# Sixteen row buffers, eight result buffers and sixteen-ahead gathers for the expert tiles, and head transposes tile by tile

## What is computed

```python
shared = silu_and_mul(x @ shared_gate_up_w.T) @ shared_down_w.T   # 704 wide
shared = shared * sigmoid(x @ shared_gate_w.T)
probs = softmax(x @ gate_w.T)
weights, chosen = top_k(probs, 2)
for e in range(8):
    w_e = where(chosen == e, weights, 0).sum(-1)
    combined += w_e[:, None] * (silu_and_mul(x @ w13[e].T) @ w2[e].T)   # 176 wide
out = shared + combined
```

## Time and profile before

| | us |
|---|---|
| median of 3 launches | 1727.43 |
| lowest and highest launch | 1725.33, 1733.93 |
| the profiled execution, its own time | 1732.21 |
| its span in the profile | 1730.4 |
| PE busy | 1476.0 (85%) |
| PE weight loads | 1110.5 (64%) |
| DVE busy | 912.3 (53%) |
| ACT busy | 754.0 (44%) |
| POOL busy | 411.3 (24%) |
| mean granted TensorE clock, share of full speed | 0.939 |

### The profile page before, as it was taken

One profiled execution on the slowest core, in us unless ns is written; L12 is line 12 of the kernel. 1 busy time (PEld: TensorE's weight loads), 2 busy tenths in 40 slices (PEclk: granted clock), 3 DMA queues, 4 the chain that ended last, 5 costly groups with the idle time before them and its releaser, 6 DMA issues. The chain is left out here.

```text
span 1730.4 us, 27960 instructions
## 1 busy us (share of the span) xinstructions
PE 1476.0 (85%) x10106; PEld 1110.5 (64%) x10112; DVE 912.3 (53%) x1968; ACT 754.0 (44%) x1872; POOL 411.3 (24%) x328
## 2 busy tenths in 40 slices
PE   6999999995799789999899879878887787898587
PEld 4777787874576667767676657665555566533466
DVE  5766665663731846565555563176554314376712
ACT  5565656561334333433434434433443342586242
POOL 2607061210235221110201014520000451100162
PEclk9999999997899899999999989988897898899699
DMA  4002020100612400010000051230003223000423
GB/s 145 29 13 80 2 92 2 55 2 20 227 52 78 143 13 31 0 42 0 12 30 1 1 206 55 77 103 1 1 1 137 94 77 99 1 1 1 180 87 116
DMA packets 42996, 99.88 MB, mean 58 GB/s; under 512 B 7168, under 2 KB 21760, under 8 KB 42752
## 3 DMA queue, kind: packets, MB, share of 16 engines
q1 hardware_dynamic: 32736, 69.85, 11.8%
q0 software_dynamic: 9984, 28.32, 5.0%
q10 hardware_dynamic: 160, 0.13, 0.0%
HBM read 79.93 MB, written 18.35 MB: 57 GB/s over the span
## 5 line engine op out<-in xcount | busy, mean ns | idle before, releaser
L829 DVE TENSOR_TENSOR s_h_e<-s_bank,s_silu_e 128x176 f32<-128x176 f32 x92 | 31.4, 341 | 221.9 <-ACT s_silu_e L616 209.7
L484 PE MATMUL s_bank<-s_expert_w,s_xe 128*128 x368 | 130.5, 479 | 0.8 <-ACT s_xe L610 0.7
L508 PE MATMUL s_bank<-s_expert_w,s_he 88*128 x368 | 97.7, 387 | 30.6 <-ACT s_he L622 30.6
L356 POOL DMA_INDIRECT expert_rows<-s_y,s_to_row x92 | 91.3, 992 | 126.2 <-ACT s_y L628 114.3
L124 POOL TENSOR_SCALAR ln_var<-ln_moments 128x4 f32<-128x4 f32 x16 | 4.2, 260 | 492.3 <-DVE ln_moments L117 369.4
L349 POOL DMA_INDIRECT s_xg<-normed_rows,s_from_row x92 | 92.2, 1002 | 119.9 <-DVE s_from_row L744 93.1
L508 PEld LDWEIGHTS s_bank<-s_expert_w,s_he 88*128 88x128 f32 x368 | 68.4, 191 | 62.3 <-issue 43.7
L2555 POOL TENSOR_TENSOR s_w_hi<-s_w_raw,zero 128x1024 fp32r<-128x1024 f32 x25 | 55.3, 2213 | 220.6 <-PE s_memory L80 188.0
L1160 ACT ACTIVATE s_scratch<-s_bank,s_neg_max 128x128 f32<-128x128 f32 (+3 forms) x128 | 67.2, 528 | 89.2 <-DVE s_neg_max L1250 89.2
L1250 DVE TENSOR_REDUCE s_neg_max<-s_bank 128x1 f32<-128x128 f32 (+3 forms) x128 | 59.7, 488 | 74.2 <-PE s_bank L1063 74.1
L1080 PE MATMUL s_bank<-s_probs_t,s_v 128*128 128x512 f32 (+3 forms) x256 | 76.3, 441 | 20.2 <-ACT s_probs_t L1168 20.2
(11 more groups left out here) (386 smaller groups left out, 4294.7 us busy)
## 6 DMA issues: line engine op xcount, KB each, us to landing
s_expert_w<-in_experts SPq DMA_DIRECT2D x32, 608.0 KB, 12.9
s_w_raw<-in_wa_o SPq DMA_DIRECT2D x16, 512.0 KB, 4.2
s_yg<-expert_rows SPq DMA_DIRECT2D x32, 256.0 KB, 4.6
s_raw<-in_shared SPq DMA_DIRECT2D x16, 384.0 KB, 6.9
normed_rows<-s_ln_xn POOLq DMA_DIRECT2D x8, 512.0 KB, 9.5
s_w_raw<-in_wa_k SPq DMA_DIRECT2D x4, 512.0 KB, 3.9
s_w_raw<-in_wa_v SPq DMA_DIRECT2D x4, 512.0 KB, 3.5
s_w_raw<-in_wa_q SPq DMA_DIRECT2D x4, 512.0 KB, 4.9
```

The lines of the kernel that those rows point to most:

```text
L356: pool.indirect_dma_start(out=y_rows[:, :], out_offset=bass.IndirectOffsetOnAxis(ap=to_row[:, i:i + 1].bitcast(U32), axis=0), in_=y[:, i % ...
L484: last = pe.matmul(u_bank[i % 2][:, 0:2 * INTER], xe[:, i % 2, x], expert_of(P, i, w), start=c == 0, stop=c == DC - 1, skip_group_check=True)
L508: last = pe.matmul(y_bank[i % 2][:, 0:D], he[0:IHALF, i % 2, h], expert_of(IHALF, i, w), start=c == 0, stop=c == 1, skip_group_check=True)
```

## The change

It has two parts. In the expert stages the ring `xg` grows from 8 to 16 buffers and `y` from 4 to 8, in all four of them; POOL issues 16 gathers before the first scatter in the two gated stages and, as before, 8 in the two ungated ones. In the head of every stage PE waits tile by tile and transposes both column chunks of a tile before it goes to the next one; a bank's `turned` increment stands at its last transpose as before.

```diff
--- before.py
+++ after.py
@@ -33,7 +33,7 @@
 EXP_DOWN = 2 * DC * INTER
 EXP_COLS = EXP_DOWN + 2 * D
 ROWS = TOP_K * NT
-XG_RING, Y_RING = 8, 4
+XG_RING, Y_RING, AHEAD = 16, 8, 8
 AT_ORDER = P
 AT_OWNER = AT_ORDER + 2 * N_EXP * N_EXP
 AT_SLOT = AT_OWNER + TILES * N_EXP
@@ -192,13 +192,14 @@
         return DC * (half + 1)
 
     def tensor(self, pe):
-        for k in range(NHALF * DC):
-            h, c = divmod(k, DC)
-            pe.wait_ge(self.normed, (h + 1) * TB)
+        for h in range(NHALF):
             for j in range(TB):
-                last = pe.transpose(self.banks[k][:, j * P:(j + 1) * P],
-                                    self.xn[:, h * TB + j, c * P:(c + 1) * P], self.res.ident[:])
-            last.then_inc(self.turned, 1)
+                pe.wait_ge(self.normed, h * TB + j + 1)
+                for c in range(DC):
+                    last = pe.transpose(self.banks[h * DC + c][:, j * P:(j + 1) * P],
+                                        self.xn[:, h * TB + j, c * P:(c + 1) * P], self.res.ident[:])
+                    if j == TB - 1:
+                        last.then_inc(self.turned, 1)
 
     def high_part(self, act, k):
         act.wait_ge(self.turned, k + 1)
@@ -359,12 +360,13 @@
 
             pool.wait_ge(x_stored, 16 * NHALF)
             pool.wait_ge(rows_known, 1)
-            for i in range(XG_RING):
+            ahead = XG_RING if early else AHEAD
+            for i in range(ahead):
                 gather(i)
             for i in range(TILES):
                 scatter(i)
-                if i + XG_RING < TILES:
-                    gather(i + XG_RING)
+                if i + ahead < TILES:
+                    gather(i + ahead)
         @block.tensor
         def _(pe):
             def fill(bank, column, n, half):
```

## The result

Over 20 launches of each the changed kernel takes 1734.63 us (1725.52 to 1744.31), the kernel before 1727.45 (1720.85 to 1738.38). The ratio is 1.0034, with a 95% interval of 1.0018 to 1.0051: 6 us slower, a small loss, where 12.9 us of gain were forecast. It lies 20 us above the forecast and 7 above the top of the range.

What follows compares the result with a forecast made beforehand. PE, busy 85% of the span, was taken as the bound, with its late signals stalling tiles. Loops 10.4 plus heads 2.5 gave 12.9 us off 1727.4: 1714.5 us, chance 0.60, range 1706 to 1728 for 8 in 10.

Steps and rivals of the forecast that it cites:

- The gated loops: Gated stages' tile loops: tiles 3 and 6 stay late, 2.49 us each from tile 7; gains 5.0 and 5.4 us.
- The cover of the moved gathers: Gated stages before scatter 0: eight moved gathers take 10.3 us of POOL's 18.98 us wait, leaving 8.7; no cost.
- the dense run of POOL's transfers: Expert loops: POOL's gapless scatter-gather alternation, not a buffer, goes with ACT's stalls before `y_out`; path unnamed.
- The slower rival: Gated stages' shared-expert run: moved gathers delay DVE and PE behind it, up to 10.3 us a stage; 1732 us, chance 0.08.
- Rings: Larger rings in all four expert stages: no row shows a ring wait, so they were costed at nothing.
- Ungated stages unchanged: Sign to look for in the two ungated expert stages: unchanged, with five late tiles each.
- The ring rival: All four expert stages: eight result buffers remove the stalls, 34 + 2.5 = 36.5 us gained, 1691 us; chance 0.08.
- The stalls as such: Four expert loops: about every third tile comes 1.7 us late, about 20 times, about 34 us of the run.
- The heads: All eight stage heads: PE transposes tile by tile and starts sooner; 2.5 us gained in sum, bounds 0 and 7.8.
- the early products: PE's first product after the transposes: 0.8 us earlier in the wide stage, 0.7 recurrent, 0.1 in each gated stage.
- within half a per cent: Whole kernel: time neither under 1718.8 nor over 1736.1 us, about what a measurement can tell from no change; chance 0.33.

Runs made afterwards that it cites:

- `pool_busy_b`: Kernel before, plus eight POOL memsets of 128x896 straight after the eight gathers in the gated stages; repeated on a chip with late tiles: ratio 1.0013.
- `rings_alone_b`: Kernel before with 16 row and eight result buffers, still eight gathers ahead everywhere and old head transposes; repeated on a chip with late tiles: ratio 1.0016.
- `heads_alone_b`: Kernel before with only the head transposes by tile, old rings and gathers; repeated on a chip with late tiles: ratio 0.9994.
- `paced_heads`: Whole change, but the moved eight gathers go in pairs behind signals of the shared run, against the kernel before, chip with late tiles: ratio 0.9933.
- `again`: The changed kernel unaltered, run once more for a second profile, against the kernel before, on a chip without late tiles: ratio 0.9998.
- `heads_alone`: Kernel before with only the head transposes by tile, old rings and gathers, on a chip without late tiles: ratio 0.9993.

## Why the prediction was wrong

**The gated loops: right.** Tiles 3 and 6 late (3, 6 and 7 in the first stage), then 2.49, gains of 4.7 and 5.6 us for 5.0 and 5.4. In 16-ahead kernels on chips with late tiles the loops repeat at 56.4 to 57.0.

**The cover of the moved gathers: the step that failed.** "Their cover is POOL's wait of 18.98 us" looked only at POOL. The cover was there, and scatter 0 wasn't late by it. But the moved gathers lengthen an unbroken run from 8 to 16 in a place where PE, ACT and DVE hand each other signals. The cost was put at nothing. The heads lost 7.6 and 9.2 us in the changed kernel (8.0 and 7.4 behind the first gather), and 7.1, 7.4, 8.4 and 8.2 in two others with 16 in a row. With the loops' 10.3 that is a net loss of 4 to 6.5 us, where 1.0034 is 5.9. The prediction had the two halves of this in hand: it took the dense run of POOL's transfers as what goes with late signals in the loop, and it made the run in the shared part twice as long. It never put them together.

**The slower rival: the right place and nearly the price, the wrong mechanism.** It said 1732 for a loss in the shared run over 6.5 us a stage, with a chance of 0.08. That its price is near is luck. It had DVE blocked by gathers, and DVE's rows keep their lengths: in the changed kernel DVE stands idle for the 4.98 us before 489.10, while ACT and DVE wait for PE.

The Trainium skill, SBUF — State Buffer, "SBUF: two separate sides", says that a DVE operation with two SBUF inputs and a GpSimd operation that reads SBUF share a port pair as a lock, and that the one that starts first blocks the other. The traces agree in one direction: the fourth gather, which starts while such an operation runs, takes 1.70 to 1.72 us in every gated stage, and a later one 1.36 to 1.46 in some profiles. The DVE operation keeps its 0.96 us, beside the fourth gather and where it starts during a gather. `pool_busy_b` is no test of this lock, since a memset reads nothing from SBUF. What speaks against the lock as the cause is DVE's idle time. The prediction also misread rows here: the gathers at 471.71 and 478.76 in the kernel before stand beside L671, which has two SBUF inputs as well, and take 0.97 and 1.01 us, so the one at 472.98 isn't the only one beside such an operation.

**Rings: right**, at nothing. "Ungated stages unchanged": they varied, 60.0 to 62.3, with old and new rings alike. The ring rival is out: larger rings leave the late tiles, and `rings_alone_b` comes to 1.0016.

**The stalls as such.** The working priced 34 us of late tiles as a property of the kernel. They are a property of the chip or of its condition: of the six chips that the experiments ran on three showed them in every profile, three in none, and both profiles of the first comparison have them.

**The heads: the early products nearly right, the gain not shown.** PE's first transpose comes 0.45 us after the first normalisation, as forecast. PE's first product comes sooner after it by 0.7 us in the wide stage for a forecast of 0.8, in all five kernels with the new order. In the changed kernel's timeline of the wide head:

```profile
585.19 1.35 DVE L162 TENSOR_SCALAR s_ln_xn<-x,ln_moments,ln_rstd 128x256 f32<-128x256 f32 x4
...
591.00 0.47 PE L78 MATMUL s_bank<-xn_t_hi,s_w_hi 128*128 128x512 f32 x1 [1.72 <-DVE s_w_lo L1221]
```

The recurrent head gives 0.9 us in the changed kernel, where 0.7 was forecast, the first gated one 0.08 and the last one 0.23, and the two grouped attention heads nothing. The sum is some 1.9 us for 2.5. What PE does behind its first product decides what is left of that. Times of 0.9994 and 0.9993 are 1.0 and 1.2 us for 2.5, and neither interval excludes 0 or 2.5. In the gated stages the sign is even the other: heads of 59.3 to 60.1 us in `heads_alone_b`, `paced_heads` and `again`, 57.3 and 59.5 in `heads_alone`, against 57.3 to 58.9, once 59.9, in kernels with the old transposes and no late signals. The difference lies ahead of the first gather. The windows of the first 20 us of the first gated stage (busy PE, granted clock, DMA share, GB/s), kernel before:

```profile
440.31:460.31 20.00, 16.91 (x80) 0.77 1.02 386
```

and `heads_alone_b`:

```profile
437.77:457.77 20.00, 17.20 (x69) 0.60 1.01 384
```

A mean of 0.60 is 16 us of the 20 at 1.2 GHz, 0.77 is 9. This doesn't come each time, but the time goes with it. Of the ten gated heads with the new transposes eight have a mean of 0.60 to 0.71 in these 20 us and take 30.1 to 31.0 us to the first gather. Two have 0.80, the changed kernel's first gated stage and that of `heads_alone`, and take 28.2 and 28.1. With the old transposes the mean is 0.72 to 0.83, and all but two of these heads take 28.2 to 29.2. So the new order costs some 2 us in most gated heads, which the prediction had at a gain of 0.1. Why PE stays at the lower level was not tested by itself.

**Range and chances.** Everything but 0.08 of the chance sat on outcomes of at most 1728, and the range ended there. The chance of 0.33 for "within half a per cent" held the outcome, from the wrong side. The unexplained path ("I can't name the path by which it holds up PE's signal") should have widened it: whoever can't name a mechanism doesn't know what else it will do.

## What to carry to other kernels

When work is moved into an engine's idle time, ask not only whether the idle time is long enough but what runs beside it: sixteen indirect transfers in a row cost 7.0 to 8.5 us a stage here beside a chain PE, ACT, DVE that hands over every few us, on chips that show late signals, and nothing on the others. Break such a run by waits on signals that come late enough to make a gap (look at the trace whether they do); here gaps turned a loss of 0.3% into a gain of 0.7%. And before stalls are priced, look at a profile from a second chip.

## What the runs showed of the hardware

- On some chips PE's signals reach ACT and DVE late (a wait of 5.75 to 6.50 us in place of 2.19) while POOL issues indirect transfers without a pause; on others not, with the same kernel. The kernel before took 1697.84, 1699.35 and 1699.49 us on three chips without late tiles and 1727.23 to 1732.76 on three with them. One of these ran in two separate calls and showed them both times. Whether it is the chip, its neighbours' load or the recording of the profile itself on that chip isn't settled; no run tried it.
- In the shared run it can be followed at ACT's copy of the weights after the third slice (L570 to L576). That waits 1.41 to 1.42 us on the chips without late tiles. On the others it waits 1.58 to 1.74 with eight gathers ahead, and 2.94 to 3.12 (once 2.27) where the ninth and tenth follow at once. The cost to the stage is 0.6 us at twelve in a row and 7.0 to 8.5 at sixteen, and the last late signal comes within 2.3 us of the run's end. Memsets on POOL and loads by SP don't cause it.
- The length of the run isn't the whole rule. In the loop of the first gated stage before, POOL had stood 18.98 us, and the signal for tile 3 is late by the sixth transfer. Eight gathers in the shared run cost nothing that can be seen.
- Near the end of such a run PE's own matmuls stand apart too in three of the six stages, by 0.33 to 1.12 us with no releaser shown.
- The bracket "remote" in a row of ACT or DVE was most often the sign of it: a wait for PE whose matmuls had ended by the trace long before. Some late ones are put down to PE, "issue" or a DMA.
